# Own orders in the drain, small loads on SyncE's queue, and a last expert with fetched sums and plain scatters

## What is computed

```python
x = emb[tokens] * sqrt(256) + pos_enc
h = softmax(x wq (x wk)^T / 16, axis=1) (x wv)
# mixer, on layernorm(h): projections z, xBC, dt; causal convolution of 4 taps; silu; state-space scan in chunks of 128
y = (Y_diag + Y_off + D * xs) * silu(z)
h = h + rmsnorm(y) @ out_proj_w.T + (the mixer's input)
# experts, on layernorm(h): 8 experts, 2 of them per token, at most 1024 tokens per expert
scores = softmax(xf @ w_router); top 2 -> slot of each token in each of its experts
y_e = gelu(xb_e @ w1_e) @ w2_e
h = h + (sum over the token's experts of weight * y_e) + bias
```

## Time and profile before

| | us |
|---|---|
| median of 3 runs | 956.3 (954.59 to 956.98) |
| profiled execution, device time | 954.65 |
| its span in the trace | 952.7 |
| TensorE busy in the span | 912.4 (96%) |
| VectorE / ScalarE / GpSimd busy | 641.6 / 529.8 / 499.2 |
| mean granted TensorE clock | 0.985 of full |

### The profile page before, as it was taken

The page is one execution under the profiler, slowest core; times in us unless marked ns, Lnnn a source line. Parts: engine busy times, 40 slices in busy tenths (PEclk is TensorE's granted clock), DMA queues, the critical chain, the costliest instruction groups (busy, mean ns, idle before and its releaser), DMA issues. The chain is left out here.

```text
span 952.7 us, 17809 instructions
## 1 busy us (share of the span) xinstructions
PE 912.4 (96%) x5876; PEld 815.6 (86%) x5876; DVE 641.6 (67%) x1689; ACT 529.8 (56%) x1094; POOL 499.2 (52%) x493
## 2 busy tenths in 40 slices
PE   5999999999999999999998989999999999999994
PEld 5888888888888888888887889999999999999993
DVE  1577899888988898889887544646464646463640
ACT  1567777677667766776776234445444544444430
POOL 5457776887678767876677321222323223323332
PEclk8999999999999999999999989999999999999997
DMA  7920011001000000000000035344343334342221
GB/s 232 320 76 11 35 44 35 22 33 33 13 22 13 23 13 23 13 24 12 14 12 26 2 115 138 74 101 95 83 109 73 105 72 105 72 108 28 26 40 28
DMA packets 48677, 57.68 MB, mean 61 GB/s; under 512 B 6224, under 2 KB 44219, under 8 KB 48640
## 3 DMA queue, kind: packets, MB, share of 16 engines
q1 hardware_dynamic: 33568, 41.05, 13.4%
q0 software_dynamic: 13632, 15.97, 10.3%
q10 hardware_dynamic: 1440, 0.17, 0.1%
HBM read 33.09 MB, written 29.75 MB: 66 GB/s over the span
## 5 line engine op out<-in xcount | busy, mean ns | idle before, releaser
L651 POOL DMA_INDIRECT out<-ye,tok_slot x60 | 103.0, 1717 | 263.7 <-DMA out<-ye,tok_slot 138.2
L899 ACT ACTIVATE hf<-bank 128x512 f32<-128x512 f32 x128 | 79.3, 620 | 199.5 <-PE bank L1654 199.5
L1286 DVE TENSOR_TENSOR h_lo<-hf,h_hi 128x512 fp32r<-128x512 f32 x128 | 88.8, 694 | 106.2 <-ACT h_hi L901 106.2
L1652 PE MATMUL bank<-w_hi,h_hi 128*128 128x256 f32 x512 | 146.1, 285 | 0.0
L1653 PE MATMUL bank<-w_lo,h_hi 128*128 128x256 f32 x512 | 144.9, 283 | 0.0
L1654 PE MATMUL bank<-w_hi,h_lo 128*128 128x256 f32 x512 | 144.9, 283 | 0.0
L1045 DVE SCALAR_TENSOR_TENSOR xc<-bank,cw,xc 128x253 f32<-128x253 f32 (+2 forms) x288 | 128.3, 471 | 1.7
L1652 PE MATMUL bank<-xe_hi,w_hi 128*128 128x512 f32 x256 | 99.9, 390 | 0.0
L1653 PE MATMUL bank<-xe_lo,w_hi 128*128 128x512 f32 x256 | 99.8, 390 | 0.0
L1654 PE MATMUL bank<-xe_hi,w_lo 128*128 128x512 f32 x256 | 99.7, 389 | 0.0
L597 POOL DMA_INDIRECT slots_dram<-rows,slot x64 | 63.5, 993 | 66.9 <-DVE slot L1174 50.7
(11 more groups left out here) (209 smaller groups left out, 2354.0 us busy)
## 6 DMA issues: line engine op xcount, KB each, us to landing
w_raw<-w SPq DMA_DIRECT2D x16, 1024.0 KB
slots_dram<-zero_row SPq DMA_DIRECT2D x1, 8320.0 KB, 30.4
xe<-slots_dram SPq DMA_DIRECT2D x15, 520.0 KB, 3.9
out<-hb SPq DMA_DIRECT2D x16, 256.0 KB, 2.1
w_raw<-in_wT SPq DMA_DIRECT2D x1, 1288.0 KB, 6.3
slots_dram<-rows,slot POOLq DMA_INDIRECT x64
out<-ye,tok_slot POOLq DMA_INDIRECT x64, 3.8
xe<-slots_dram SPq DMA_DIRECT2D x2, 260.0 KB, 3.0
```

Source lines behind the costliest of these rows:

```text
L651: g.indirect_dma_start(out, bass.IndirectOffsetOnAxis(ap=tok_slot[q][:, j:j + 1], axis=0), ye[q][:, j, :], None, compute_op=ALU.add).then_ ...
L899: sc.activation(hf[m % 2][:, :], h_bank[i % H_BANKS][:, :], ACT.Gelu_apprx_tanh)\
L1286: vc.tensor_tensor(h_lo[:, m, :], hf[m % 2][:, :], h_hi[:, m, :].bitcast(F32), ALU.subtract)\
L1652: te.matmul(out_, hi, rhi, start=first_, stop=False)
```

## The change

Five things. SyncE issues the ten small loads, in another order, behind `w_out`; GpSimd waits for them only ahead of its product with `nw`, and splits `w_in` in two halves. In the last half with a front, GpSimd makes `gated_root` between its two `segment_inputs`, and VectorE doesn't call `residual`. The drain's half with `b` has an order of its own on each engine, in which `residual(t, p)` stands behind the first `decay_scores`. The numbers of `keep_clock` differ, and ten small products ahead of the experts are gone. In the last expert all eight tiles are gathered, and all eight are written with plain scatters; VectorE adds the first four in one instruction.

```diff
+        FILL = dict(t=3, scores=2, attend=5, hT=18, dt=8)
+        DRAIN = dict(state=2, seg0=3, seg1=2, seg2=2, own=2, yT0=2, yT1=2, out=2)
+        LAST = dict(v2T=19, route=2, choices=8)
@@ SyncE, behind the load of w_out
+            for dst, src in small:
+                sp.dma_start(dst, src).then_inc(s_small, 16)
@@ GpSimd, start
-            pool.wait_ge(s_small, 16 * N_SMALL)
             pool.wait_ge(s_win, 16)
-            g.tensor_copy(w_in_hi[:, :, :], w_in).then_inc(w_in_split, 1)
+            for k in range(KD):
+                g.tensor_copy(w_in_hi[:, k, :], w_in[:, k, :]).then_inc(w_in_split, 1)
...
             pool.wait_ge(s_wout, 16)
+            pool.wait_ge(s_small, 16 * N_SMALL)
@@ GpSimd, half
+                if not f:
+                    if b:
+                        decayed_x(b, q)
+                        skip_x(b, q, 0)
+                        second_root(t, p)
+                        skip_x(b, q, 1)
+                        with_bias(t, p)
+                        describe_rows(t, p)
+                        gated_root(b, q)
+                        second_root(b, q)
+                    else:
+                        with_bias(t, p)
+                        describe_rows(t, p)
+                    scatter_rows(t, p)
+                    free_rows(t, p)
+                    return
...
+                if not nf:
+                    segment_inputs(f, p, 0)
+                    gated_root(b, q)
+                    segment_inputs(f, p, 1)
+                    free_rows(t, p)
+                    with_bias(t, p)
+                    return
@@ GpSimd, last expert
+                for j in range(JS):
+                    g.indirect_dma_start(base[:, j, :], None, out,
                                          bass.IndirectOffsetOnAxis(ap=tok_slot[1][:, j:j + 1], axis=0))\
+                        .then_inc(fetched[j * 2 // JS], 16)
...
+                pool.wait_ge(summed_up, 1)
+                for j in range(JS):
+                    if j >= JS // 2:
+                        hold(pool, ye_ready, 2 + JS * (NE - 1) + j + 1)
                     g.indirect_dma_start(out, ..., ye[1][:, j, :], None).then_inc(added, 16)
                     pool.wait_ge(added, 16 * (JS * (NE - 1) + j + 1))
@@ ScalarE, start
-            act.wait_ge(gathered[0], gathered.per_turn)
-            for dst, src in small:
-                act.dma_start(dst, src).then_inc(s_small, 16)
@@ ScalarE, half
+                if b and not f:
+                    silu_conv(b, q, 0)
+                    silu_conv(b, q, 1)
+                    silu_z(b, q, 0)
+                    silu_conv(b, q, 2)
+                    silu_z(b, q, 1)
+                    state_inputs(b, q)
+                    x_rows(b, q, 0)
+                    decay(b, q, 0)
+                    decay(b, q, 1)
+                    end_decay(b, q)
+                    x_rows(b, q, 1)
+                    decay(b, q, 2)
+                    decay(b, q, 3)
+                    state(b, q)
+                    norm_2(t, p)
+                    transposed_rows(t, p)
+                    transposed_y(b, q, 0)
+                    router_exp(t, p)
+                    transposed_y(b, q, 1)
+                    squares(b, q)
+                    return
@@ VectorE, half
+                if b and not f:
+                    mask_scores(b, q)
+                    times_dt(b, q, 0)
+                    decay_scores(b, q, 0)
+                    residual(t, p)
+                    times_dt(b, q, 1)
+                    decay_scores(b, q, 1)
+                    first_y(b, q)
+                    carried_y(b, q)
+                    second_y(b, q)
+                    router_in(t, p)
+                    router_top(t, p)
+                    mean_square(b, q)
+                    residual(b, q)
+                    slots_of(t, p)
+                    count_choices(p)
...
-                if b:
+                if b and nf:
                     residual(b, q)
@@ VectorE, last expert, behind the tiles of group 2
+                    if last and g == 2 * NG - 2:
+                        dve.wait_ge(fetched[0], 16 * (JS // 2))
+                        dve.wait_ge(ye_ready, 2 + JS * (NE - 1) + JS // 2)
+                        vc.tensor_tensor(ye[1][:, 0:JS // 2, :], ye[1][:, 0:JS // 2, :], base[:, 0:JS // 2, :], ALU.add)\
+                            .then_inc(summed_up, 1)
@@ TensorE, half
+                if b and not f:
                     project_z(b, q, 0)
                     project_z(b, q, 1)
                     keep_clock(p, DRAIN["state"])
                     state_inputs(b, q)
                     x_to_rows(b, q, 0)
+                    keep_clock(p, DRAIN["seg0"])
+                    segment_sums(b, q, 0)
+                    keep_clock(p, DRAIN["seg1"])
+                    segment_sums(b, q, 1)
+                    x_to_rows(b, q, 1)
+                    keep_clock(p, DRAIN["seg2"])
+                    segment_sums(b, q, 2)
+                    segment_sums(b, q, 3)
+                    chunk_state(b, q)
+                    keep_clock(p, DRAIN["own"])
+                    own_chunk(b, q, 0)
+                    to_v2T(t, p)
+                    from_state(b, q)
+                    keep_clock(p, DRAIN["own"])
+                    own_chunk(b, q, 1)
+                    keep_clock(p, DRAIN["yT0"])
+                    to_yT(b, q, 0)
+                    route(t, p)
+                    keep_clock(p, DRAIN["yT1"])
+                    to_yT(b, q, 1)
+                    keep_clock(p, DRAIN["out"])
+                    project_out(b, q)
+                    choices_before(t, p)
+                    return
...
-            keep_clock(0, 32)
+            keep_clock(0, 38)
             pe.wait_ge(part_done, 1)
             pe.sem_inc(y_psum, Y0)
-            for _ in range(10):
-                te.matmul(bank[0][1][:, 0:P], ident[0:32, :], ident[0:32, :], start=True, stop=True)
...
-                    keep_clock(0, 9)
+                    keep_clock(0, 6)
```

More of the change, by code:

```diff
@@ L361, in lm_block @@
         added = sem("added")
-        fetched = sem("fetched")
+        fetched = [sem(f"fetched{n}") for n in range(2)]
+        summed_up = sem("summed_up")
         expert_added = sem("expert_added")
@@ L380, in lm_block @@
         XS_BANK, YD_BANK, YT_BANK = (2, 1), (1, 0), (3, 1)
-        FILL = {'t': 3, 'scores': 2, 'attend': 5, 'hT': 18, 'dt': 8}
-        DRAIN = {'state': 2, 'seg0': 3, 'seg1': 4, 'v2T': 4, 'seg2': 2, 'seg3': 2, 'own': 2, 'yT0': 2, 'yT1': 2, 'out': 1}
-        LAST = {'v2T': 20, 'route': 2, 'choices': 6}
+        FILL = dict(t=3, scores=2, attend=5, hT=18, dt=8)
+        DRAIN = dict(state=2, seg0=3, seg1=2, seg2=2, own=2, yT0=2, yT1=2, out=2)
+        LAST = dict(v2T=19, route=2, choices=8)
         PER_TURN = 2 * NG * KF
@@ L616, in half @@
                     skip_x(b, q, 1)
-                if f and not final:
+                if not final:
                     gather_next(f, p)
@@ L660, in fetch_sums @@
             def fetch_sums():
[L662 to L663 removed]
+                for j in range(JS):
+                    g.indirect_dma_start(base[:, j, :], None, out,
                                          bass.IndirectOffsetOnAxis(ap=tok_slot[1][:, j:j + 1], axis=0))\
[L665 to L666 removed]
+                        .then_inc(fetched[j * 2 // JS], 16)
+                for part in fetched:
+                    pool.wait_ge(part, 16 * (JS // 2))
             def write_sums():
[L670 to L673 removed]
+                pool.wait_ge(summed_up, 1)
+                for j in range(JS):
+                    if j >= JS // 2:
+                        hold(pool, ye_ready, 2 + JS * (NE - 1) + j + 1)
                     g.indirect_dma_start(out, bass.IndirectOffsetOnAxis(ap=tok_slot[1][:, j:j + 1], axis=0),
@@ L1542, in half @@
                 q = 1 - p
-                filling, draining = not b and not t, not f
-                if filling:
+                if b and not f:
+                    project_z(b, q, 0)
+                    project_z(b, q, 1)
+                    keep_clock(p, DRAIN["state"])
+                    state_inputs(b, q)
+                    x_to_rows(b, q, 0)
+                    keep_clock(p, DRAIN["seg0"])
[21 more added lines that the diff above has]
+                    choices_before(t, p)
+                    return
+                if not f:
+                    keep_clock(p, LAST["v2T"])
+                    to_v2T(t, p)
+                    keep_clock(p, LAST["route"])
+                    route(t, p)
+                    keep_clock(p, LAST["choices"])
+                    choices_before(t, p)
+                    return
+                if not b:
                     keep_clock(q, FILL["t"])
@@ L1555, in half @@
                     scores(f, p)
-                if b and draining:
-                    keep_clock(p, DRAIN["state"])
                 if b:
@@ L1593, in half @@
                     chunk_state(b, q)
-                if b and draining:
```

(15 more changed lines are left out.)

81 lines of the change are left out of this document (24 added, 57 removed).

## The result

The kernel after takes 948.25 us (median of 9 executions, 946.58 to 951.88), the kernel before beside it 956.82 (953.38 to 959.41, 9). The ratio is 0.9922 with a 95% interval of 0.9899 to 0.9944: 0.8% faster, 7.5 us by the ratio. 949.1 was forecast. The profiled execution took 951.88, with a span of 950.1, and so is the slowest of the nine; the others lie in two groups, 946.58 to 948.70 and 951.68 to 951.88. It also means that the traced execution after is a slow one: its span is only 2.6 us shorter than the traced one before (952.7), so most of the 7.5 us lies in executions of which there is no trace.

What follows compares the result with a forecast made beforehand. TensorE was taken to bound the experts' loop, busy 200 us of 200, so only fill, drain, passage and end could move: 1.2 + 2.2 + 0.9 + 2.9 = 7.2 us off 956.3 gives 949.1, range 946 to 952.

Steps and rivals of the forecast that it cites:

- Fill: Pipeline start: small loads moved to SyncE let `tT` start 2.0 us earlier; less 0.8 for the clock, 1.2 saved.
- The clock term: Pipeline start: slow scores product behind TensorE's idle gap costs 1.6 us more; half charged, 0.8.
- Drain: End of the token pipeline: own orders start `own_chunk` 0 3.7 us earlier and `project_out` 2.2 earlier; 2.2 saved.
- both theories: Orders: each part saves what its chain of waits says. Clock: new TensorE idle gaps slow products, giving gains back.
- the lower end: Token pipeline's drain: 0 saved if GpSimd gets the port first (1.25 us) and the clock falls again (1.1 us).
- Passage: From token pipeline to experts: fewer clock products bring the first product at 565.4; 0.9 us saved, at most 1.3.
- End: Last expert: eight gathers and eight plain scatters issue the last scatter earlier; 2.9 us saved, between 0.7 and 4.2.
- the stall of 1.1: Last expert's scatters: half of the delay behind a plain scatter landing after 4.6 us, charged once.
- The rival of slow plain scatters: GpSimd's chain of eight: 5.43 us period beside a busy core gives 963.4, or 956.9 if only five slow; chance 0.10.
- The clock rival: Half clock behind new TensorE gaps: fill 0, passage -0.6, drain 1.1, end 2.9; 3.4 us saved, 952.9; chance 0.18.
- One part cancelled: Small loads land after 20.8 or GpSimd holds the drain's port: 1.2 or 2.2 us lost, 950.3 to 951.3; chance 0.12.

Runs made afterwards that it cites:

- warm_fill: Changed kernel with 26 unused clock products instead of 2 ahead of the first scores; 949.56 us, ratio to the kernel before 0.9939.
- warm_all: Changed kernel with clock products: 26 ahead of first scores, 8 ahead of `chunk_state`, 12 behind `part_done`, 10 instead of 6 behind the transposes; 945.26 us.
- warm_all_nohold: warm_all, with the last four scatters waiting for `ye_ready` plainly, without the count that `hold` adds on GpSimd; 942.43 us, ratio to the kernel before 0.9866.
- warm_drain: Changed kernel with 8 unused clock products ahead of `chunk_state` in the drain; 947.94 us, ratio to the kernel before 0.9923.
- fill_alone: Kernel before with only the fill's part: SyncE issues ten small loads, `w_in` split in halves, later wait for `w_out`'s factor; 954.64 us, ratio 0.9983.
- before_warm_drain: Kernel before with 14 clock products instead of 4 between its first and second segment sum; 954.55 us, ratio 0.9979.
- pass_alone: Kernel before with only the passage's part: 38 clock products instead of 32 ahead, no ten small products, 6 instead of 9 behind the transposes; 954.17 us.
- end_alone: Kernel before with only the end's part: eight gathers, eight plain scatters, one VectorE addition over 1024 elements; 953.53 us, ratio 0.9972.
- after_again: The changed kernel once more, unaltered, for a second profile and more times; 950.10 us, ratio to the kernel before 0.9935.
- drain_alone: Kernel before with only the drain's part: own orders of all queues and the `keep_clock` numbers in DRAIN and LAST; 951.05 us, ratio 0.9941.
- end_late_gathers: Changed kernel with gathers 5 to 8 of the last expert held back until the fourth `ye` is ready; 955.10 us, ratio to the kernel before 0.9986.
- warm_pass: Changed kernel with 12 clock products behind `part_done` and 10 instead of 6 behind the transposes; 951.54 us, ratio to the kernel before 0.9944.

## Why the prediction was right, and where its steps were not

949.1 was forecast, 948.25 and 950.10 were measured. The sum is right, in part by luck. The layouts behind the drain and the passage hold where the clock is full; the end came out by errors that cancel; and in the fill, the drain and the passage of the traced executions half clock took back more than I had charged. Nor do the traces show the sum: the traced pair differs by 2.6 us. Against before, after has `project_out` 1.0 later behind `a_lo`, 0.1 more from there to the load of `xe`, 0.9 less from it to the first product, 0.5 more from there to the last `ye`, 3.9 less from it to the last scatter, and 0.5 more behind that.

**Fill, 1.2 forecast.** The steps to `tT` hold: `bias_b` landed at 18.65 (18.8 forecast), `tT` at 18.81 (19.1). `wqk` was ready far sooner than I thought, at 9.8 and not at 12 to 13, because ScalarE's table load moved too, from 15.09 to 0.81, with no DMA issue in front of it. So TensorE finished the query product by 12.9 and idled 6.11 instead of 4 to 5. The clock term was mis-sized: I charged 0.8, the scores alone cost 1.8 (3.78 against 1.99), the way from `tT` to `v` 1.5 to 2.4 in all, and `v` gained some 0.5. With the gap filled, `tT` to `v` is 4.71 or 4.72 (warm_fill, warm_all, warm_all_nohold), as with the old start, and `v` came at 24.69 and 23.80 in the first two, 1.6 and 2.5 ahead of the old mean of 26.28: at full clock the shift of `tT` reaches `v` unshortened. Behind `v` the way to `a_lo` in the drain varies by 1.2 us from trace to trace (482.4 to 483.6), so only means show what arrives there: `a_lo` at 509.2 with the old start (five), 508.9 with the new one unfilled (six), 507.5 filled (three).

**Drain, 2.2 forecast.** The layout was near exact where the clock let it be. Counted from `a_lo` (508.74 before, 508.86 in warm_drain), I had 13.7 for the first own chunk and 23.0 for `project_out`, and warm_drain shows 13.49 and 22.89. The second segment sum is at 514.86, and the 5.36 us ahead of `rows` are gone. VectorE got ahead of GpSimd as laid out: `seg` from 516.55 to 518.41, and GpSimd's `hb` beside it took 2.25 us where it took 1.27 before. The distance from `a_lo` to `project_out` tells both theories apart:

| drain | granted clock in it | `a_lo` to `project_out`, us |
|---|---|---|
| old order: fill_alone, before_warm_drain | full | 25.64, 25.63 |
| old order: before, pass_alone, end_alone | half for a while (mean 0.96 from 500 to 540) | 25.63, 26.48, 26.66 |
| new order: after_again, drain_alone, end_late_gathers | half for a while (0.91) | 25.56, 25.57, 25.37 |
| new order: after, warm_fill, warm_pass | half for longer (after: 0.87) | 26.59, 26.38, 26.43 |
| new order: warm_drain, warm_all, warm_all_nohold | full | 22.89, 22.90, 22.89 |

At full clock the new order saves 2.7; with the fall in it, its 25.4 to 26.6 is where the old one stands (25.6 to 26.7). That is the step that failed: the forecast has nothing for the clock, and the lower end 1.1 us for a fall in the gaps. It falls on the own chunk, 8 products (16 passes) on the path right behind the gap (1.6 us), and on what follows it: 2.5 to 3.7 in all. The fall is not certain in each execution: the unfilled kernel has the two groups of times, 947 to 949 and 951 to 952, and warm_drain only the lower. That the lower group kept its clock in the drain is inferred from its mean granted clock (0.987 to 0.991 against 0.984 to 0.986) and from warm_drain. The arithmetic fits: outside the drain after's trace has 20.7 us at half clock, which alone would make a mean of 0.989. A trace of such an execution there is not.

In the drain the trace shows half clock behind 2.10 us of idle, in the passage behind 4.52. The Trainium skill (TensorE: Matmul & The Clock Gate, "What's actually happening") says that the slow clock is the default and activity releases it; the three traces with 8 calls of unused products in the drain's gap, all at full clock there, agree.

**Passage, 0.9 forecast.** The distance that I gave as 8.7 was 8.53 in the trace. It became 7.66, 7.60 and 7.55 (after, pass_alone, after_again): 0.9, and alone 1.6 by the ratio with an interval from 0.1 to 3.2. Behind the first product after and after_again give 0.5 back to the clock, so there the term is 0.4 to 0.5; pass_alone, with 372.25, keeps it whole. Full clock brings the distance to 6.99 and 6.92 (warm_all, warm_all_nohold). The old passage was not always 8.5 either: in fill_alone it took 9.92, in before_warm_drain 7.52 and in end_alone 7.51. The mean of the five traces with the old passage is 8.4, that of the six with the new one and nothing filled there 7.6.

**End, 2.9 forecast.** The last scatter was to start at 941.7 + 1.1 = 942.8 and started at 942.68, but by other steps. (The first product is only 0.3 later than before, so these instants can be set side by side.) The first one came at 921.53 and not at 919.1, because of the late `ye`: 2.4 lost. The seven periods took 21.15 instead of 7 x 3.23 = 22.6: the first three have no count ahead and took 2.92, 2.69 and 2.66: 1.5 gained. And the stall of 1.1 that I charged did not come. The rival of slow plain scatters falls: beside a busy TensorE the period is 2.7 to 3.2 where the landing is not late, and the mean of the seven is in no kernel near 4.8. (In that rival four scatters, not five, are issued before 939; the sum has four.) The 14 profiles hold 92 plain scatters of the last expert. Three landed after 4.3 to 4.6 us (one each in before, fill_alone and warm_pass), one after 3.5 (warm_fill), all others within 2.7. How much the part saves depends on that. The last scatter stands behind the last `ye` by 7.26, 7.08, 6.41, 5.13 and 4.60 in the five profiles with the old end, the first two with a landing over 4 us; by 3.38, 3.16, 3.74, 4.17, 3.48, 3.69 and 6.61 in those with the new end (and `hold`, and gathers in a row), the last one with such a landing. With all counted that is 6.1 against 4.0, without those landings 5.4 against 3.6: 1.8 to 2.1, of which the longer tail takes 0.5. The traces so show 1.3 to 1.6 and not 2.9. end_alone has 2.7 by the ratio, with an interval from 1.3 to 4.1, so these agree only at its lower end.

**The clock rival, 0.18.** It was half right. It forecast 952.9; the upper group, three of nine executions and four of eight, lies at 951 to 952. Its terms were not those of the traces: it had nothing for the fill, where `v` gained 0.5; 0.6 lost in the passage, where 0.4 to 0.5 was gained; and 1.1 gained in the drain, where the six traces with half clock in the new order lie between 0.3 gained and 1.0 lost against the 25.63 of before.

**One part cancelled, 0.12.** Neither of its causes came: the small loads landed by 18.65, not after 20.8, and GpSimd did not go first in the drain. What cancelled the drain in the traced executions was the clock.

**What stays open.** The parts alone sum to 11.5 us, the whole gives 6.2 to 7.5. The intervals of the parts reach 1.3 to 1.8 us to either side, so some of that may be chance, but drain_alone at 5.6 is twice the 2.7 that its orders gave in a profile at full clock. That executions of the kernel before lose clock in places that its one profile doesn't show would fit, and that profile is of a quick execution (954.65, where the medians beside the other runs are 956.1 to 956.8); it is only argued. Nor were the orders of the single engines separated within drain_alone.

## What to carry to other kernels

When an order is made tighter, TensorE's idle time gathers in one gap, and what stands right behind that gap decides the gain: look at the granted clock there, and fill the gap with unused products up to the instant at which the wait ends. Compare two orders at the same clock, by the distance from a mark that no order touches, and not by one profile's total: here single executions of one kernel lie 5 us apart. In a chain of transfers that each wait for the one before, count what the issuing engine does between landing and issue; one semaphore count per link was 0.55 us of 3.22.

## What the runs showed of the hardware that was not expected

- The times of single executions go with TensorE's mean granted clock in each kernel that has unfilled gaps: in the kernel before from 951.93 us at 0.989 to 959.17 at 0.982, in drain_alone from 948.71 at 0.988 to 954.60 at 0.982. In warm_drain (0.989 to 0.992) they lie within 1.0 us. Filling all three gaps does not rule a fall out: one execution each of warm_all and warm_all_nohold stands 2 to 3 us above the others, at 0.993 (the others 0.995 to 0.998). Part of the mean is the idle end of the kernel, where the clock is at half as well.
- A VectorE operation that reads PSUM was held up by a row of GpSimd's gathers. In after the third `ye` waited from about 914.0 until 917.26. A running gather alone does not stop it: the `ye` before it was on time and started beside one in after_again (910.52, the gather from 910.38 to 911.33) and in warm_pass (911.28, from 911.25 to 912.20). The Trainium skill (SBUF — State Buffer, "Who interferes with whom") says that a VectorE instruction with at most one SBUF input, outside the two-port modes, does not contend with GpSimd. By that rule the `ye` would have gone on time; the trace shows otherwise, and end_late_gathers shows that the gathers are the cause. By which way, a port, the load of an instruction or a late semaphore, no run here tells. TensorE was not delayed: from its first product to the last `ye` it is 372.2 us with the late `ye` too (end_alone 372.24, before 372.22).
- GpSimd's count on a semaphore ahead of an indirect scatter costs 0.55 us (0.83 from landing to issue against 0.27).
- Plain indirect scatters of 128 rows land in 2.4 us beside a busy core and beside an idle one; 3 of 92 took over 4, without a cause that the traces show.
